# One more fp32 matmul per edge step on TensorE, ahead of the wait for the step's rows, in the passes of layers 1 to 3 of a four-layer graph network

## The chip, the cores and the metric

One core of one Trainium2 chip. The metric is the device time of one launch, in microseconds (us); lower is better.

## The reference, cut to what matters

A graph of 6250 nodes with 256 features and 100000 edges goes through four layers, each followed by a residual sum and a layer norm:

```python
x = _layernorm(x + _L0_gnn_ref(x, edge_index, ...))            # attention, 8 heads
x = _layernorm(x + _L1_gnn_ref(x, edge_index, ...))            # two GCN convolutions, 512 hidden
x = _layernorm(x + _L2_gnn_ref(x, edge_weight, ..., src, dst)) # edge-weighted convolution
x = _layernorm(x + _L3_gnn_ref(x, edge_index, edge_attr_2, ...)) # attention, 4 heads of 64
```

What matters here is the sum over edges in each layer: a row of a node table is fetched by the edge's source, weighted, and added to the row of the edge's destination.

```python
msg = h[src] * norm[:, None]
return jax.ops.segment_sum(msg, dst, num_segments=n_nodes) + b
```

The edges are sorted by destination. All arithmetic is float32.

## The kernel before, in words

Nodes are cut into 49 tiles of 128 (NODE_TILES). Edges are cut into 782 chunks of 128 (CHUNKS). A step pairs one chunk with one tile of destinations; since edges are sorted, 782 + 48 = 830 steps (STEPS) cover all pairs. The sums of all nodes lie in reg_acc, the features of all nodes in reg_x (as x_sb, tile by tile).

There are five passes over the edges. Layer 0 has its own (heads_*, product at L957); the change does not touch it. Layer 1 has two (edges1 and edges2) and layer 2 one (edges3); these three are instances of the class EdgePass (L1085 to L1152). Layer 3 has the last one (mix_*, L1494 to L1662). Dense layers and norms stand between the passes (close0 to close4), and each pass begins when the table that it gathers from has been stored.

One pass of EdgePass, engine by engine:

- POOL (L1099) issues one indirect DMA per chunk, 782 in all, each fetching 128 rows of 256 features into a ring of 60 slots. Gather j waits for the product of step j - 12 (AHEAD is 60 - 48 = 12), because a slot may be needed by up to 48 later steps.
- ACT (L1107) makes the one-hot matrix of a step (128 edges x 128 nodes) in two operations, four steps at a time (L1111 and L1116), in a ring of 12. In edges3 DVE makes it (L1136) with the edge weight in it.
- PE (L1118) multiplies: one fp32 matmul per step, one-hot x rows, 256 columns, into one of 8 PSUM banks (L1130). Before the product of step i it waits for the one-hot, for gather i (only if i < 782), and, from step 8 on, for the add of step i - 8, which frees the bank. The last 48 steps of a pass have no gather of their own.
- DVE (L1139) adds the bank into the tile's sums (L1152), each add behind the one before it.

The order of each engine is the order of its loop; nothing else schedules the work.

The last pass has 832 steps (STEPS_PAD), in 52 groups of 16:

- POOL (L1499) gathers rows of 136 columns by step, in a ring of three groups; gather t waits for the message of step t - 48.
- DVE at step i weights the message by head (L1651, after the product of step i - 4), mixes the message of step i + 1 (L1620), does a piece of the next group's score chain (chain, L1577; it begins by waiting for the last gather of the next group, L1583), and adds the product of step i - 2 to the sums (L1639). At the start of a group it rescales the sums (L1631 and L1633).
- ACT (L1555) makes the one-hots and the reversed messages and copies the weights.
- PE (L1517) does one product per step, 260 columns (L1526), into one of 6 banks, and two small operations per group for the running maximum (L1509, L1512). Before a product it waits for the one-hot, the weighted message, the weights, and the add of step i - 6.

An fp32 matmul leaves two records in the trace, so 830 products are 1660 records, and "x8" of PE's L153 or L1130 are four matmuls. A few records of PE are missing.

Of the kernel before, what the change touches and what calls it, by code (L numbers as in the profile page):

```python
# [46 lines left out]
EDGE_BANKS = 8  # L47
BANKS = 6
LAG = 2
ROW_OF_SLOTS = 32  # L50
NI, NF = 4, 3


# [159 lines left out]
def build(nc, io):  # L213
    ctx = ExitStack()
    with ctx:
        def sb(name, width, dt=F32, rows=P):
            return ctx.enter_context(nc.sbuf_tensor(name, [rows, width], dt))
# [21 lines left out]
        attr1 = sb("attr1", STEPS_PAD)  # L239
        step_rows = sb("step_rows", STEPS_PAD, I32, rows=ROW_OF_SLOTS + 1)  # L240
        tile_row, slot_row = step_rows[0:1, :], step_rows[ROW_OF_SLOTS:ROW_OF_SLOTS + 1, :]
        group_row = sb("group_row", NODE_TILES, I32, rows=1)
        ident = sb("ident", P)
# [4 lines left out]
        psum = [ctx.enter_context(nc.psum_tensor(f"bank{k}", [P, 512], F32)) for k in range(8)]  # L248
# [11 lines left out]
        x_sb = reg_x[:, 0:NODE_TILES * FEAT].rearrange("p (t f) -> p t f", f=FEAT)  # L260
# [381 lines left out]
        def load_slots(e, t0):  # L642
            if not slot_regs:
                slot_regs.extend(e.alloc_register(f"slot{k}") for k in range(GROUP))
            n = min(GROUP, STEPS - t0)
            e.load(slot_regs[0:n], slot_row[:, t0:t0 + n])

        def slot_rows(e, t):
            v = e.snap(slot_regs[t % GROUP], min_val=0, max_val=(SLOTS - 1) * FEAT)
            return scratch[:, bass.DynSlice(v, FEAT)]  # L650
# [428 lines left out]

        ring_rows = scratch[:, 0:SLOTS * FEAT].rearrange("p (s f) -> p s f", f=FEAT)
        ring_hots = scratch[:, SLOTS * FEAT:SLOTS * FEAT + HOTS * P].rearrange("p (s f) -> p s f", f=P)

        class EdgePass:  # L1085
# [32 lines left out]
            def tensor(self, e):  # L1118
                for i in range(STEPS):
                    if i % GROUP == 0:  # L1120
                        load_slots(e, i)
                    if self.weighted:
                        e.wait_ge(*self.hot(i))
                    else:
                        e.wait_ge(*self.hot4(i // 4))
                    if i < CHUNKS:
                        e.wait_ge(*self.got[i % AHEAD](i // AHEAD))
                    if i >= EDGE_BANKS:
                        e.wait_ge(*self.added(i - EDGE_BANKS))
                    e.matmul(psum[i % EDGE_BANKS][:, 0:FEAT], ring_hots[:, i % HOTS, :], slot_rows(e, i),  # L1130
                             start=True, stop=True).then_inc(*self.product.up)

# [345 lines left out]
        product3, added3 = s_edge.take(STEPS_PAD), s_added.take(STEPS_PAD)  # L1478
        scaled_3, denscaled3 = s_scaled.take(GROUPS - 1), s_denscaled.take(GROUPS - 1)

        def close3_over(e):

            e.wait_ge(*h3_stored.end)
            e.wait_ge(*src_by_step.end)
            e.wait_ge(*cleared_l2.end)
            e.wait_ge(*norm_l2.scaled.end)
            e.wait_ge(*dense_l3.turned.end)
            e.wait_ge(*taken_l3.end)
# [14 lines left out]
        def mix_tensor(e):  # L1503
            close3_over(e)

            def chain(g, k):
                if k == 4:
                    e.wait_ge(*cm_v.at("top", g))
                    e.transpose(top_bank[0:HEADS3, 0:P], top, ident[:, :]).then_inc(*cm_t.done("top"))  # L1509
                if k == 9:  # L1510
                    e.wait_ge(*cm_v.at("diag", g))
                    e.matmul(top_bank[:, 256:256 + HEADS3], ones4, diag, start=True,  # L1512
                             stop=True).then_inc(*cm_t.done("all"))

            for k in range(GROUP):
                chain(0, k)
            for i in range(STEPS_PAD):  # L1517
                g, k = i // GROUP, i % GROUP
                if g + 1 < GROUPS:
                    chain(g + 1, k)  # L1520
                e.wait_ge(*hot3(i // 4))
                e.wait_ge(*weighted3(i))
                e.wait_ge(*wkept3(i))
                if i >= BANKS:
                    e.wait_ge(*added3(i - BANKS))
                e.matmul(psum[i % BANKS][:, 0:WIDE3], hots3[:, i % 12, :], scaled3[:, i % 4, :], start=True,  # L1526
                         stop=True).then_inc(*product3.up)

# [217 lines left out]
        @block.tensor  # L1746
        def _(e):
            prep_tensor(e)
            heads_tensor(e)
            edges1.tensor(e)  # L1750
            close1_tensor(e)
            edges2.tensor(e)
            close2_tensor(e)
            edges3.tensor(e)
            close3_tensor(e)
            mix_tensor(e)
# [102 lines left out]
```

## Time and profile before

| | us |
|---|---|
| median of 3 runs | 6089.86 |
| lowest and highest of them | 6069.24, 6090.07 |
| the profiled execution's own time | 6087.99 |
| its span, first to last instruction | 6086.2 |

From the profiled execution, busy time and share of the span by engine:

| engine | busy us | share | instructions |
|---|---|---|---|
| PE (matmul) | 4655.6 | 76% | 13320 |
| POOL | 4038.2 | 66% | 4116 |
| DVE | 3512.5 | 58% | 10769 |
| ACT | 2590.8 | 43% | 7522 |

PE is TensorE's matmuls and PEld its weight loads; DVE is VectorE, ACT ScalarE, POOL GpSimd. Busy time of PE depends on its clock: the granted clock is given as a share of 2.4 GHz, so 1.00 is 2.4 GHz and 0.50 is 1.2 GHz; its mean over the span is 0.696. Matmuls overlap each other, and a record shows a matmul's whole way through the array; the distance between the starts of two tells the rate. In the timeline a line merges like instructions that follow each other closely, and the bracket behind it tells how long the engine was idle before it and what ended that.

The pass edges1 lies from 1375 to 2389 us, edges2 from 2609 to 3623, edges3 from 3746 to 4760, and the last pass from 4858 to 6002.

### The profile page before, as it was taken

To read this page: it belongs to the slowest core of one execution; us is meant where nothing else is said; L and a number is where in the kernel's file an instruction comes from. 1 tells how busy PE (TensorE), PEld (TensorE's weight loads), DVE (VectorE), ACT (ScalarE), POOL (GpSimd) and SP (SyncE) were. 2 spreads that over 40 slices of the span, in tenths; PEclk is the share of its full clock that TensorE was granted. 3 is DMA by queue.
4 is the path that set the end of the run, shared out by engine and by line. 5 is a ranking of instruction groups with operands and counts; after the bars stand their busy time and mean duration, and the time that the engine had idled before them with its cause. 6 is when DMAs were issued, how large, how long until landed. Compare 5 with 4: busy or idle time off the path is not lost.

```text
span 6086.2 us, 70752 instructions
## 1 busy us (share of the span) xinstructions
PE 4655.6 (76%) x13320; PEld 2535.9 (42%) x13320; DVE 3512.5 (58%) x10769; ACT 2590.8 (43%) x7522; POOL 4038.2 (66%) x4116
## 2 busy tenths in 40 slices
PE   5899988837888888988888863887888856666663
PEld 3667666623333334633333331333333623333331
DVE  4767787783333335833333347555555767777777
ACT  1655566554444444444444453000000456666664
POOL 2776677727777773067777755777777177777772
PEclk8877798775655667966565665656565977777776
DMA  4433343334333331033333322333333122222221
GB/s 128 107 106 96 96 107 107 101 96 119 105 105 106 106 105 50 33 105 106 106 105 105 106 62 82 105 106 105 105 105 105 36 54 53 53 53 53 53 53 55
DMA packets 237655, 539.07 MB, mean 89 GB/s; under 512 B 68266, under 2 KB 120424, under 8 KB 237242
## 3 DMA queue, kind: packets, MB, share of 16 engines
q0 software_dynamic: 180176, 481.36, 29.2%
q1 hardware_dynamic: 57066, 53.19, 2.7%
q8 instruction: 140, 2.29, 0.2%
q14 instruction: 273, 2.24, 0.1%
HBM read 498.15 MB, written 36.14 MB: 88 GB/s over the span
## 4 chain that ended last, share of the span: by engine, by line
PE 64%; issue 14%; DVE 12%; ACT 5%; POOL 2%; DMA 1%; DVEq 1%; ACTq 0%; POOLq 0%
PE bank L1130 40%; PE bank L1526 10%; PE bank L957 8%; PE bank L814 4%; PE bank L802 2%; DVE reg_acc L1152 1%; DVE scratch L183 1%; DVE scratch L201 1%; POOL scratch L1103 1%; DVE reg_acc L985 1%; ACT scratch L1541 1%; DVE scratch L1242 1%; ACT scratch L1546 1%; DVE scratch L1245 1%; DVE scratch L1233 1%
## 5 line engine op out<-in xcount | busy, mean ns | idle before, releaser
L1130 PE MATMUL bank<-scratch 128*128 x4980 | 2582.2, 634 | 668.3 <-issue 279.3
L1152 DVE TENSOR_TENSOR reg_acc<-reg_acc,bank 128x256 f32 x2490 | 1049.6, 422 | 1803.2 <-PE bank L1130 1779.7
L1130 PEld LDWEIGHTS bank<-scratch 128*128 128x128 f32 x4980 | 1147.9, 281 | 2102.5 <-issue 2077.3
L1103 POOL DMA_INDIRECT scratch<-tab_x,src_idx x1564 | 1479.5, 946 | 513.9 <-issue 383.8
L1111 ACT ACTIVATE scratch<-iota_row,dst_loc 128x128 f32<-128x128 f32 x1660 | 660.7, 401 | 1084.7 <-PE bank L1130 1066.0
L1103 POOL DMA_INDIRECT scratch<-tab_h,src_idx x782 | 739.3, 945 | 494.6 <-DMA tab_h<-reg_acc 256.7
L1499 POOL DMA_INDIRECT scratch<-tab_h,src_idx x832 | 856.1, 1029 | 263.8 <-issue 162.1
L710 POOL DMA_INDIRECT reg_x<-tab_h,src_idx x832 | 809.4, 973 | 301.0 <-issue 174.3
L1526 PE MATMUL bank<-scratch 128*128 128x260 f32 x1664 | 676.8, 525 | 425.9 <-issue 403.9
L957 PE MATMUL bank<-reg_x,scratch 128*128 128x265 f32 x1664 | 639.8, 495 | 102.3 <-DVE reg_x L994 60.5
L1526 PEld LDWEIGHTS bank<-scratch 128*128 128x128 f32 x1664 | 326.7, 242 | 743.4 <-issue 702.3
L146 ACT COPY scratch<-bank 128x256 f32<-128x256 f32 (+1 forms) x196 | 76.8, 416 | 1035.0 <-PE bank L138 1035.0
L957 PEld LDWEIGHTS bank<-reg_x,scratch 128*128 128x128 f32 x1664 | 317.2, 227 | 245.4 <-DVE reg_x L994 215.6
L985 DVE TENSOR_TENSOR reg_acc<-reg_acc,bank 128x265 f32 x832 | 355.0, 427 | 100.4 <-PE bank L957 87.0
L994 DVE TENSOR_TENSOR reg_x<-reg_x 128x256 f32<-128x256 f32 x832 | 349.8, 421 | 0.4 <-ACT reg_x L767 0.4
L1639 DVE TENSOR_TENSOR reg_acc<-reg_acc,bank 128x260 f32 x832 | 341.4, 410 | 9.4 <-DVE reg_acc L1633 7.7
L1651 DVE TENSOR_TENSOR scratch<-scratch 128x256 f32<-128x256 f32 x832 | 342.8, 412 | 0.0
L1541 ACT ACTIVATE scratch<-iota_row,dst_loc 128x128 f32<-128x128 f32 x832 | 320.5, 386 | 0.0
L1136 DVE TENSOR_SCALAR scratch<-iota_row,dst_loc,edge_w 128x128 f32<-128x128 f32 x830 | 291.8, 352 | 0.0
L1564 ACT COPY scratch<-scratch 128x4 f32<-128x4 f32 x832 | 152.4, 183 | 326.4 <-PE bank L1526 321.3
L1552 ACT ACTIVATE scratch<-scratch,attr 128x64 f32<-128x64 f32 x832 | 285.9, 344 | 1.0 <-issue 0.9
L814 PEld LDWEIGHTS bank<-adst,scratch 128*128 128x128 f32 x1664 | 269.4, 241 | 38.6 <-issue 32.4
(229 smaller groups left out, 4430.7 us busy)
## 6 DMA issues: line engine op xcount, KB each, us to landing
scratch<-tab_h,src_idx POOLq DMA_INDIRECT x1614, 2.7
scratch<-tab_x,src_idx POOLq DMA_INDIRECT x1564, 2.7
reg_x<-tab_h,src_idx POOLq DMA_INDIRECT x832
reg_x<-in_x SPq DMA_DIRECT2D x12, 896.0 KB, 11.0
tab_h<-scratch SPq DMA_DIRECT2D x7, 924.0 KB, 4.5
tab_x<-reg_acc SPq DMA_DIRECT2D x7, 896.0 KB
tab_h<-reg_acc SPq DMA_DIRECT2D x7, 896.0 KB
tab_x<-reg_x SPq DMA_DIRECT2D x7, 896.0 KB
```

Of the source, the lines that this page charges most:

```text
L710: e.indirect_dma_start(rows0[:, t % (3 * S), 0:ROW0], None, tab_h0, bass.IndirectOffsetOnAxis(ap=src_idx[:, t:t + 1], axis=0)).then_inc(*g ...
L814: m = e.matmul(bank_d[:, t % S * H:(t % S + 1) * H], hots_t[:, c % 2, n * P:(n + 1) * P], adst[:, bass.DynSlice(tile_value(e, "tensor", t) ...
L957: e.matmul(psum[i % BANKS0][:, 0:W0_ROW], hots0[:, i % (2 * S), :], rows0[:, i % (3 * S), :], start=True, stop=True).then_inc(*product0.up)
L985: e.tensor_tensor(v, v, psum[i % BANKS0][:, 0:W0_ROW], ALU.add).then_inc(*added0.up)
L994: e.tensor_tensor(v, v, bcast(row[:, FEAT:ROW0], 2, [P, H, D]), ALU.mult).then_inc(*weighted0.up)
L1103: e.indirect_dma_start(ring_rows[:, j % SLOTS, :], None, self.table, bass.IndirectOffsetOnAxis(ap=src_idx[:, j:j + 1], axis=0)).then_inc(* ...
L1111: e.activation(ring_hots[:, i % HOTS, :], iota_row[:, :], ACT.Abs, scale=-1.0, bias=dst_loc[:, i:i + 1]).then_inc(*self.far.up)
L1130: e.matmul(psum[i % EDGE_BANKS][:, 0:FEAT], ring_hots[:, i % HOTS, :], slot_rows(e, i), start=True, stop=True).then_inc(*self.product.up)
L1152: e.tensor_tensor(v, v, psum[i % EDGE_BANKS][:, 0:FEAT], ALU.add).then_inc(*self.added.up)
L1499: e.indirect_dma_start(rows3[:, t % (3 * GROUP), :], None, tab_h3, bass.IndirectOffsetOnAxis(ap=src_idx[:, t:t + 1], axis=0)).then_inc(*go ...
L1526: e.matmul(psum[i % BANKS][:, 0:WIDE3], hots3[:, i % 12, :], scaled3[:, i % 4, :], start=True, stop=True).then_inc(*product3.up)
L1541: e.activation(hots3[:, i % 12, :], iota_row[:, :], ACT.Abs, scale=-1.0, bias=dst_loc[:, i:i + 1]).then_inc(*far3.up)
```

## The change

Each step of the three EdgePass passes from step 8 on, and of the last pass from step 6 on, gets one more matmul on PE: the identity matrix times the first 384 columns of x_sb (the node features, resident and unchanged during a pass), written to the bank that the step's product then overwrites (start=True). Its result is taken by nobody. The wait for the bank (the add of 8 or 6 steps before) moves from last to first among the step's waits, so that the new matmul can run before the step's one-hot and rows are there. The constant FILL0 is not used.

```diff
 BANKS = 6
 LAG = 2
 ROW_OF_SLOTS = 32
+FILL = 384
+FILL0 = 160
...
+        def busy_beside(e, bank, rows):
+
+            e.matmul(bank, ident[:, :], rows.rearrange("p t f -> p (t f)")[:, 0:FILL], start=True, stop=True)
+
...
                 for i in range(STEPS):
                     if i % GROUP == 0:
                         load_slots(e, i)
+                    if i >= EDGE_BANKS:
+                        e.wait_ge(*self.added(i - EDGE_BANKS))
+                        busy_beside(e, psum[i % EDGE_BANKS][:, 0:FILL], x_sb)
                     if self.weighted:
                         e.wait_ge(*self.hot(i))
                     else:
                         e.wait_ge(*self.hot4(i // 4))
                     if i < CHUNKS:
                         e.wait_ge(*self.got[i % AHEAD](i // AHEAD))
-                    if i >= EDGE_BANKS:
-                        e.wait_ge(*self.added(i - EDGE_BANKS))
                     e.matmul(psum[i % EDGE_BANKS][:, 0:FEAT], ring_hots[:, i % HOTS, :], slot_rows(e, i),
                              start=True, stop=True).then_inc(*self.product.up)
...
                 if g + 1 < GROUPS:
                     chain(g + 1, k)
+                if i >= BANKS:
+                    e.wait_ge(*added3(i - BANKS))
+                    busy_beside(e, psum[i % BANKS][:, 0:FILL], x_sb)
                 e.wait_ge(*hot3(i // 4))
                 e.wait_ge(*weighted3(i))
                 e.wait_ge(*wkept3(i))
-                if i >= BANKS:
-                    e.wait_ge(*added3(i - BANKS))
                 e.matmul(psum[i % BANKS][:, 0:WIDE3], hots3[:, i % 12, :], scaled3[:, i % 4, :], start=True,
                          stop=True).then_inc(*product3.up)
```

## Rows read from the trace of the kernel before

**Rows 1.** The page: busy time by engine, and the chain by line.

```profile
PE 4655.6 (76%) x13320; PEld 2535.9 (42%) x13320; DVE 3512.5 (58%) x10769; ACT 2590.8 (43%) x7522; POOL 4038.2 (66%) x4116
...
PE bank L1130 40%; PE bank L1526 10%; PE bank L957 8%; PE bank L814 4%; PE bank L802 2%; DVE reg_acc L1152 1%; DVE scratch L183 1%; DVE scratch L201 1%; POOL scratch L1103 1%; DVE reg_acc L985 1%; ACT scratch L1541 1%; DVE scratch L1242 1%;
```

**Rows 2.** Stretches: length, busy time of each engine, granted clock, DMA share, GB/s.

```profile
core 0: us, PE busy (x) PEld busy (x) DVE busy (x) ACT busy (x) POOL busy (x), PEclk, DMA share, GB/s
1390.00:2350.00 960.00, 819.84 (x1537) 359.65 (x1537) 323.83 (x769) 426.52 (x960) 726.06 (x769) 0.60 0.37 105
1436.00:1444.00 8.00, 7.62 (x14) 3.39 (x14) 2.95 (x7) 3.52 (x9) 6.12 (x7) 0.50 0.39 110
1444.00:1452.00 8.00, 6.33 (x14) 2.40 (x12) 2.77 (x7) 3.77 (x9) 5.92 (x7) 0.73 0.36 100
2356.00:2389.50 33.50, 26.28 (x96) 15.79 (x95) 20.65 (x49) 18.88 (x47) 0.00 (x0) 0.96 0.00 1
2400.00:2590.00 190.00, 187.79 (x805) 128.30 (x804) 165.41 (x321) 91.45 (x225) 0.00 (x0) 1.00 0.09 30
```

**Rows 3.** Groups in 1390:2350: busy us, mean ns; idle before, releasers.

```profile
L1130 PE MATMUL bank<-scratch 128*128 x1537 | 820.6, 647 | 140.7 <-issue 102.6 <-ACT scratch L1116 13.1 <-DVE reg_acc L1152 7.5
L1103 POOL DMA_INDIRECT scratch<-tab_x,src_idx x769 | 727.0, 945 | 234.2 <-issue 185.2 <-PE bank L1130 49.0
```

**Rows 4.** Timeline (start, us), ends of passes 1 and 3: POOL and DVE.

```profile
2351.78 0.95 POOL L1103 DMA_INDIRECT scratch<-tab_x,src_idx  x1 [0.30 <-issue]
...
2356.11 0.42 DVE L1152 TENSOR_TENSOR reg_acc<-reg_acc,bank 128x256 f32 x1 [0.87 <-PE bank L1130]
...
2389.07 0.42 DVE L1152 TENSOR_TENSOR reg_acc<-reg_acc,bank 128x256 f32 x1 [0.22 <-DVE reg_acc L1152]
...
4722.70 0.95 POOL L1103 DMA_INDIRECT scratch<-tab_x,src_idx  x1 [0.30 <-issue]
...
4726.46 0.42 DVE L1152 TENSOR_TENSOR reg_acc<-reg_acc,bank 128x256 f32 x1 [0.57 <-PE bank L1130]
...
4759.88 0.42 DVE L1152 TENSOR_TENSOR reg_acc<-reg_acc,bank 128x256 f32 x1 [0.22 <-DVE reg_acc L1152]
```

**Rows 5.** Timeline of PE in the dense layer behind pass 1.

```profile
2451.10 1.94 PE L153 MATMUL bank<-reg_w,scratch 128*128 128x512 f32 x4
2452.88 0.38 PE L138 MATMUL bank<-ident,reg_acc 128*128 128x128 f32 x2
2453.10 1.89 PE L153 MATMUL bank<-reg_w,scratch 128*128 128x256 f32 x8
2454.83 0.60 PE L138 MATMUL bank<-ident,scratch 128*128 128x128 f32 x4
```

**Rows 6.** Timeline, one group of the last pass: DVE and PE.

```profile
5304.94 0.22 DVE L1583 TENSOR_TENSOR scratch<-scratch,attr 128x64 f32<-128x64 f32 x1 [4.30 <-DMA scratch<-tab_h,src_idx]
...
5309.23 1.21 PE L1526 MATMUL bank<-scratch 128*128 128x260 f32 x2 [0.95 <-issue]
...
5326.31 0.23 DVE L1583 TENSOR_TENSOR scratch<-scratch,attr 128x64 f32<-128x64 f32 x1 [4.83 <-DMA scratch<-tab_h,src_idx]
```

**Rows 7.** The gathers of the last pass, 4890:6000, as in rows 3.

```profile
L1499 POOL DMA_INDIRECT scratch<-tab_h,src_idx x807 | 832.5, 1032 | 245.9 <-issue 154.8 <-DVE scratch L1620 91.1
```

**Rows 8.** Timeline later in the same group: POOL, DVE and PE.

```profile
5315.34 1.30 POOL L1499 DMA_INDIRECT scratch<-tab_h,src_idx  x1 [0.30 <-DVE scratch L1620]
5315.41 0.41 DVE L1651 TENSOR_TENSOR scratch<-scratch 128x256 f32<-128x256 f32 x1
...
5316.78 0.68 PE L1526 MATMUL bank<-scratch 128*128 128x260 f32 x2 [0.19 <-issue]
...
5316.94 0.95 POOL L1499 DMA_INDIRECT scratch<-tab_h,src_idx  x1 [0.30 <-DVE scratch L1620]
5317.21 0.41 DVE L1651 TENSOR_TENSOR scratch<-scratch 128x256 f32<-128x256 f32 x1
```

**Rows 9.** Timeline of DVE, the last two groups: their first and last instruction.

```profile
5969.30 0.22 DVE L1583 TENSOR_TENSOR scratch<-scratch,attr 128x64 f32<-128x64 f32 x1 [4.32 <-DMA scratch<-tab_h,src_idx]
...
6001.12 0.43 DVE L1639 TENSOR_TENSOR reg_acc<-reg_acc,bank 128x260 f32 x1 [0.22 <-DVE reg_acc L1639]
```

## Prediction, made before the changed kernel was run

> **What bounds the kernel now.** I read five views in this order: the page's busy times and chain, a table of stretches, the groups inside one edge pass, the timeline at the ends of the passes, and one group of the last pass. The page shows PE busiest (76%), and 40% of the chain that ended last at its line L1130 alone [rows 1]. That invites the reading that the edge passes wait for PE, and that a faster PE clock would shorten them. The stretches show what is odd about PE: through 960 us of pass 1 it is 85% busy, but at a mean granted clock of 0.60, while in the dense layer behind it the clock is 1.00, that is 2.4 GHz against 1.2 GHz at 0.50 [rows 2]. So most of PE's busy time in the passes is slowness.
>
> Who paces the pass? In the same 960 us, POOL issues 769 gathers of 945 ns each, with 234 us of gaps: 961 us, all of it [rows 3]. POOL's period is 945 + 304 = 1.25 us per step, and its gap is 0.30 us whether the releaser is "issue" or PE. Step i needs gather i, so PE does one step per 1.25 us at either clock. Does POOL itself wait for PE? Gather j needs product j-12. The add of step 781 is the 49th from the end; in pass 3 it starts at 4726.46, 3.8 us behind its gather (4722.70), in pass 1 at 2356.11, 4.3 us behind (2351.78) [rows 4]. Product j-12 was thus there 12 x 1.25 - 4.3 = 10.7 us before gather j. PE may fall 10 us behind before POOL feels it. The chain puts these steps down to PE only because PE works last in each step.
>
> The 48 last steps of a pass have no gather. They run from 2356.11 to 2389.49 at 0.69 us, and DVE paces them: an add of 422 ns and 0.22 us before the next, while PE needs only 0.43 us for a product [rows 4, 5].
>
> **The change, part by part.** Passes 1 and 2 of layer 1 and the pass of layer 2 (830 steps each) and the last pass (832 steps) get one more fp32 matmul per step, ident against 384 columns, from step 8 on (step 6 in the last pass). The wait for a free bank moves ahead of it; it asks for the add eight (six) steps back, long done in the main stretch, so the move costs nothing: only the rows' waits come after it, and if the add were late, the product would wait for it in either order.
>
> Price of the added matmul: the trace has none of 384 columns, so I take it between its neighbours. At clock 1.00 four matmuls of 256 columns take 2453.10 to 2454.83, 0.43 us each; two of 512 take 2451.10 to 2452.88, 0.89 us each (two records to a matmul) [rows 5]. Midway: 0.66 us. Bounds: 0.64 (1.5 x 0.43) and 0.89. The step becomes 0.43 + 0.66 = 1.09 us at 2.4 GHz, 2.19 us at 1.2 GHz.
>
> Which clock? 1.09 of 1.25 us is 87% busy with columns. The clock stood at 0.96 and 1.00 where PE was 78% busy (the 48 last steps) and 99% (the dense layer); where it falls again and again, in the main stretch, PE's fast step fills only 0.43 of 1.25 us (35%) [rows 2, 3, 5]. At 0.50 a step of 2.19 us would leave PE no gap at all, and behind a stretch of 95% busy at 0.50 it rises now (1436:1444, then 0.73) [rows 2]. So I take 1.00, after some microseconds at the start of a pass, in which PE falls behind by 0.43 us per us; 7 us of that are 3 us of the 10 us of slack.
>
> (1) Main stretch of three edge passes, 782 gathers each: 1.09 < 1.25, POOL goes on pacing: 0. The cover is 0.16 us per step; if it were gone (a step of 1.30 us, say), each pass would lose 782 x 0.05 = 39 us.
>
> (2) The last 48 steps: no gather to hide behind. PE needs 1.09 where DVE needed 0.69: 48 x 1.09 = 52.3 us. From the last gather to the end of the last add it is now 37.7 us in pass 1 and 37.6 in pass 3 (pass 2, the same program, is taken as alike); with the change 3.8 + 52.3 + 0.4 = 56.5. Loss: 18.9 each, **+57 us** for three [rows 4, 5]. The bounds of the price (0.64, 0.89) give +54 and +90; I keep 0.66, as 256 columns are the nearest form.
>
> (3) Last pass, main stretch. A group of 16 steps takes 21.4 us (5304.94 to 5326.31); DVE waits 4.3 and 4.8 us of it for the next group's rows: POOL paces here too [rows 6]. PE's demand: the first three steps are DVE's own (4.3 us to the product at 5309.23), then, at 1.10 for 260 columns and the fill, 13 x 1.10 = 14.3, and some 0.8 for the two small operations of a group (less than two products): 19.4 us < 21.4. The product at 5309.23 takes 1.21 us, a later one of the same group (5316.78) 0.68: the clock is low at the start of the group, behind the idle gap [rows 6, 8]; if it still falls, three steps take 6.6 instead of 4.3 us and the group 21.7. That closes the gap ahead of the next group, so it should not happen each time. Taken as 0; bound +0.3 x 51 = +15 us.
>
> (4) POOL's own pace there. Gathers last 1032 ns on average, not 945 [rows 3, 7]. The timeline says why: the gather that starts 0.07 us ahead of DVE's L1651 (5315.34 and 5315.41) takes 1.30 us, the next one, 0.27 us ahead of it (5316.94 and 5317.21), takes 0.95 [rows 8]. That costs 0.087 x 16 = 1.4 us per group. DVE's step is 0.90 us there now (5315.41 to 5317.21, two steps) [rows 8]; paced by PE it would be 1.10. A gather then shifts by 0.15 us per step against L1651, and meets the bad zone (some 0.35 us wide, an estimate from the 0.35 us by which that one is stretched) about once in five, not once in two or three: 2.7 x 0.33 = 0.9 us per group, 0.5 less. Because the first steps keep DVE's rhythm I take 0.4: **-20 us**. Bounds: 0.9 less (-45) and 0.5 more (+25), since where two rhythms lock is chance. The Trainium skill (SBUF — State Buffer, "Who interferes with whom") says a DVE instruction with two inputs in SBUF contends with a GpSimd instruction that reads SBUF, but that a tensor_tensor should leave descriptor generation alone. This trace agrees with the first half (L1651 has both inputs in SBUF; beside L1152, with one in PSUM, gathers stay at 945 ns) and not with the second; by the second alone this term would be 0 and the sum +64.
>
> (5) The last two groups have no gathers behind them: 5969.30 to 6001.55, 32.3 us [rows 9]. Then 4.3 + 29 x 1.10 + 0.8 + 0.6 = 37.6, and 2.3 if the clock is low at the start, as at 5309.23 now: **+7 us** (+5 to +8).
>
> Sum: 57 + 7 - 20 = +44. The profiled execution took 6087.99 us, 1.9 below the median of the runs shown (6089.86); so 6132 for it, 6134 for the median, 0.7% more. Each of the three runs shown lies within 21 us of the others; about 0.5% (30 us) is what a measurement can tell from no change.
>
> **Rivals.** *POOL is freed (not slower).* The extra matmul spreads DVE's L1651 so far apart that hardly any gather is stretched. All of 1.4 us in 51 groups would give back 71 us: 6090 + 64 - 71 = 6083. It decides the sign against 0.5% from 34 us on (0.67 us per group). For it: phases lock, and 0.15 us of shift is small. Against: it needs more than half of all stretches to go. *PE becomes the bound.* If the fill costs 0.89 us, a step is 1.32 and the edge passes follow PE: 3 x 782 x 0.07 = 164, with 90 for the ends: about 6340. If the clock stayed at 1.2 GHz, 2.19 us per step would add 0.94 x 2346 = 2200 us; the rise at 95% load [rows 2] speaks against it. The mild form, the last pass at PE's pace, gives 6150 to 6190. *The clock was the cost.* If the passes followed PE's slow steps, 2.4 GHz would bring PE's product from about 1.0 to 0.43 us; but POOL's 1.25 us leaves nothing to win: 0, and the ends still cost: this ends in my forecast. *It does nothing,* the ends being paced by DVE still: PE's fill would have to fit in 0.69 - 0.43 = 0.26 us; no row lets 384 columns do that.
>
> **How the numbers follow.** Forecast (ends dominate, some relief at POOL): 0.70, slower. POOL freed: 0.20, of which 0.17 within 0.5% and 0.03 faster. PE the bound somewhere: 0.07, slower. Nothing: 0.03, same. So slower 0.77, same 0.20, faster 0.03. The range goes from term (4) at its bound, 6090 + 64 - 45 = 6109, a little into the first rival (6100), to the sum with +15 of (3), +15 for a dearer step at the ends and +5 of (4): 6090 + 64 + 35 = 6189, cut to 6185 for what is unlikely together.
>
> **What would show it.** Clock near 1.00 in all passes; PE about 88% busy in the main stretches; edge gathers still 1.25 us apart, 782 in 977 us; DVE's adds 1.09 us apart in the last 48 steps, 56 us from the last gather to the end; L1651 at 1.1 us distance and fewer gathers over 1.2 us; groups of 21.0 us. Wrong would be: gathers with gaps above 0.3 us released by PE; a clock of 0.50 in the middle of a pass; the ends still at 0.69 us.

## The result, and the profile after

The changed kernel took 6129.77 us (median of 9 runs, 6085.37 to 6154.74), the kernel before beside it 6089.86 (9 runs, 6069.24 to 6111.16): ratio 1.0054, 95% interval 1.0031 to 1.0078. It is slower by 40 us in the medians, 0.65%, or 0.3 to 0.8% by the interval. The forecast was 6134, slower, +44. The profiled execution took 6137.57 us, with a span of 6135.8 and a mean granted clock of 0.927.

The page of the changed kernel: busy time by engine (rows 1 are its counterpart), and the costliest groups.

```profile
PE 5275.6 (86%) x19904; PEld 3455.7 (56%) x19904; DVE 3572.2 (58%) x10769; ACT 2622.6 (43%) x7522; POOL 4016.5 (65%) x4116
...
L1086 PE MATMUL bank<-reg_x,ident 128*128 128x384 f32 x6584 | 2681.1, 489 | 59.8 <-issue 59.5
```

L1086 is the added matmul, L1137 the edge passes' product (L1130 before), L1109 and L1159 their gather and add (L1103, L1152). In the last pass L1534 is the product, L1506 the gather, L1591 the start of the score chain and L1659 the weighting (L1526, L1499, L1583 and L1651 before). PE has 620 us more busy time, and the program is 40 us longer.

The same kernel by stretches, columns as in rows 2: the main part of pass 1 (7 us longer than the stretch in rows 2), its last steps, and the last pass.

```profile
1400.00:2367.00 967.00, 914.62 (x3097) 551.59 (x3098) 327.27 (x777) 433.79 (x971) 731.28 (x774) 1.00 0.36 106
2371.00:2423.00 52.00, 51.39 (x192) 35.97 (x190) 20.50 (x49) 20.68 (x47) 0.00 (x0) 1.00 0.00 1
4970.00:6010.00 1040.00, 915.77 (x3322) 606.34 (x3320) 816.23 (x3028) 689.44 (x2678) 798.34 (x794) 1.00 0.21 54
```

The clock is 1.00 where it was 0.60 [rows 2]. Yet POOL issues 774 gathers in 967 us, 1.25 us apart, as before. In the last steps PE, which was busy for 26.28 of 33.5 us there, is now busy for 51.39 of 52.

The gathers and the products of pass 1 in 1400:2367, columns as in rows 3.

```profile
L1109 POOL DMA_INDIRECT scratch<-tab_x,src_idx x774 | 731.6, 945 | 235.7 <-PE bank L1137 134.0 <-issue 101.7
L1137 PE MATMUL bank<-scratch 128*128 x1554 | 499.9, 404 | 31.1 <-DMA scratch<-tab_x,src_idx 27.9 <-ACT scratch L1122 1.9 <-issue 0.2
```

POOL's gap is still 235.7 / 774 = 0.30 us, whoever is named as its releaser; a record of a product now lasts 404 ns instead of 647, and PE's waits are for the rows.

The ends of passes 1 and 3, timeline of POOL and DVE: last gather, add of step 781, last add [rows 4].

```profile
2367.03 0.95 POOL L1109 DMA_INDIRECT scratch<-tab_x,src_idx  x1 [0.30 <-PE bank L1137]
...
2370.87 0.42 DVE L1159 TENSOR_TENSOR reg_acc<-reg_acc,bank 128x256 f32 x1 [0.83 <-PE bank L1137]
...
2422.55 0.42 DVE L1159 TENSOR_TENSOR reg_acc<-reg_acc,bank 128x256 f32 x1 [0.66 <-PE bank L1137]
...
4772.85 0.95 POOL L1109 DMA_INDIRECT scratch<-tab_x,src_idx  x1 [0.30 <-issue]
...
4776.62 0.42 DVE L1159 TENSOR_TENSOR reg_acc<-reg_acc,bank 128x256 f32 x1 [0.52 <-PE bank L1137]
...
4828.30 0.42 DVE L1159 TENSOR_TENSOR reg_acc<-reg_acc,bank 128x256 f32 x1 [0.66 <-PE bank L1137]
```

From the last gather to the end of the last add it is 55.9 us in both, 37.7 and 37.6 before. The 48 steps take 51.68 us, 1.077 each; the wait in front of an add is 0.66 us and named PE, where it was 0.22 us and DVE's own.

Below, the program is cut at the first and last gather and the last add of each pass. "Ends" is the time from a pass's last gather to the end of its last add, for passes 1, 2 and 3 together. "Rest" is the span without layer 0's pass, in which the change touches nothing.

| kernel | layer 0's pass (clock) | gathers of passes 1 / 2 / 3 | ends | last pass, median group | rest |
|---|---|---|---|---|---|
| before | 1149.6 (0.81) | 976.3 / 976.3 / 977.1 | 112.8 | 1143.2, 21.47 | 4936.6 |
| after | 1164.7 (0.80) | 976.1 / 976.3 / 977.1 | 167.8 | 1126.2, 20.99 | 4971.1 |

So the change costs 34.5 us in the parts that it touches: +55.0 at the ends, -17.0 in the last pass, -3.6 between passes (behind passes 1 and 3 the next pass begins 1.8 us sooner after the last add; in the first 4 us of the dense layer behind pass 1 the clock is 1.00, where it was 0.50). The other 15 us by which these two profiled executions differ lie in layer 0's pass.

### The profile page after: what moved, and what is told of

Read it like the earlier page. It is cut to its first block, busy times and chain, and to the rows that moved or that the text cites. A ratio compares the mean times of both kernels' runs of the same rounds, so it can differ in the third digit from the quotient of the medians.

```text
span 6135.8 us, 82950 instructions
## 1 busy us (share of the span) xinstructions
PE 5275.6 (86%) x19904; PEld 3455.7 (56%) x19904; DVE 3572.2 (58%) x10769; ACT 2622.6 (43%) x7522; POOL 4016.5 (65%) x4116
## 4 chain that ended last, share of the span: by engine, by line
PE 70%; DVE 9%; DMA 7%; issue 6%; POOL 3%; ACT 2%; DVEq 0%; ACTq 0%; POOLq 0%
PE bank L1086 31%; PE bank L1137 19%; PE bank L959 8%; PE bank L1534 6%; DMA scratch<-tab_x,src_idx 4%; PE bank L816 4%; DMA scratch<-tab_h,src_idx 2%; PE bank L804 2%; POOL scratch L1109 2%; DVE scratch L185 1%; DVE scratch L203 1%; DVE reg_acc L987 1%; POOL reg_x L712 1%; DVE scratch L1249 1%; DVE scratch L1252 1%
## 5 line engine op out<-in xcount | busy, mean ns | idle before, releaser
L1086 PE MATMUL bank<-reg_x,ident 128*128 128x384 f32 x6584 | 2681.1, 489 | 59.8 <-issue 59.5
L1159 DVE TENSOR_TENSOR reg_acc<-reg_acc,bank 128x256 f32 x2490 | 1048.7, 421 | 1819.6 <-PE bank L1137 1817.5
L1137 PE MATMUL bank<-scratch 128*128 x4980 | 1604.5, 404 | 335.4 <-DMA scratch<-tab_x,src_idx 283.8
L1109 POOL DMA_INDIRECT scratch<-tab_x,src_idx x1564 | 1479.4, 946 | 513.9 <-PE bank L1137 264.7
L1137 PEld LDWEIGHTS bank<-scratch 128*128 128x128 f32 x4980 | 843.4, 190 | 1315.8 <-issue 1048.9
L1086 PEld LDWEIGHTS bank<-reg_x,ident 128*128 128x128 f32 x6584 | 1233.6, 190 | 279.7 <-issue 109.0
L1109 POOL DMA_INDIRECT scratch<-tab_h,src_idx x782 | 739.3, 945 | 511.1 <-DMA tab_h<-reg_acc 273.2
L1506 POOL DMA_INDIRECT scratch<-tab_h,src_idx x832 | 835.1, 1004 | 263.8 <-issue 143.5
L1534 PE MATMUL bank<-scratch 128*128 128x260 f32 x1664 | 511.6, 390 | 142.9 <-issue 135.9
L1534 PEld LDWEIGHTS bank<-scratch 128*128 128x128 f32 x1664 | 308.9, 191 | 397.0 <-issue 226.8
L1659 DVE TENSOR_TENSOR scratch<-scratch 128x256 f32<-128x256 f32 x832 | 344.3, 414 | 0.3
L1143 DVE TENSOR_SCALAR scratch<-iota_row,dst_loc,edge_w 128x128 f32<-128x128 f32 x830 | 328.5, 397 | 0.0
```

The costliest lines, as they stand in the source:

```text
L1086: e.matmul(bank, ident[:, :], rows.rearrange("p t f -> p (t f)")[:, 0:FILL], start=True, stop=True)
L1109: e.indirect_dma_start(ring_rows[:, j % SLOTS, :], None, self.table, bass.IndirectOffsetOnAxis(ap=src_idx[:, j:j + 1], axis=0)).then_inc(* ...
L1159: e.tensor_tensor(v, v, psum[i % EDGE_BANKS][:, 0:FEAT], ALU.add).then_inc(*self.added.up)
L1506: e.indirect_dma_start(rows3[:, t % (3 * GROUP), :], None, tab_h3, bass.IndirectOffsetOnAxis(ap=src_idx[:, t:t + 1], axis=0)).then_inc(*go ...
```

## Experiments

My theory: the fill is free where a gather paces the step, and costs at the ends, where no gather does; the gain in the last pass comes from DVE's L1659, which PE's pace spreads out in time, so that it stretches fewer gathers. The rivals: the end of a pass isn't the cost, but something in the main stretch is; and the gain in the last pass comes from the clock, not from the pace.

Four sets of runs were made, each on one chip with the kernel before beside it. On the chips of two sets the kernel before took 6101.36 and 6099.73 us, on those of the other two 6997.5 and 6996.24. The first set fell on the slower kind, so its kernels but mix_only were run again (names ending in _b).

### The change again

**after_b**: no edit.

> The changed kernel itself, as a control on the chip of this call (on the chip of the runs before, the kernel before took 6998 us, and DMA paused for 1.6 to 3.3 us every 13 us or so). If this chip is like the first one (kernel before near 6090): edge passes 976 us plus 56 us each, last pass 1126 us, about 0.7% over the kernel before. If it is like the second: each edge pass loses 18 us at its end and 15 to 20 us in its main stretch, and the last pass 70 us, so some 170 us or 2.4% over the kernel before.

Measured 6139.29 us (5 runs) against 6101.36 (14): 1.0064, interval 1.0037 to 1.0091. Gathers 976.1 / 976.2 / 976.9, ends 167.9, last pass 1126.3 with groups of 20.99, rest 4971.6: within half a microsecond of the first profile. Layer 0's pass took 1138.6 (clock 0.82), 26 us less than there. So these two executions differ in layer 0's pass alone, and "rest" is the measure for what follows.

### No fill where no gather hides it

**ends_off** and **ends_off_b** (the same kernel twice): the fill stops with the last gather.

```diff
-                    if i >= EDGE_BANKS:
-                        e.wait_ge(*self.added(i - EDGE_BANKS))
-                        busy_beside(e, psum[i % EDGE_BANKS][:, 0:FILL], x_sb)
+                    if i >= EDGE_BANKS:
+                        e.wait_ge(*self.added(i - EDGE_BANKS))
+                    if EDGE_BANKS <= i < CHUNKS:
+                        busy_beside(e, psum[i % EDGE_BANKS][:, 0:FILL], x_sb)
```

> The changed kernel without the extra matmul in the last 48 steps of the edge passes. My theory: 18 us less at the end of each edge pass than the changed kernel on the same chip, 55 us in all, and nothing else changed. On a chip like the first: 37.6 us from last gather to end, and 0.2 to 0.3% below the kernel before. Rival: the extra matmuls of the main stretch cost something too, and the total stays above the kernel before.

ends_off_b: 6073.14 us (10 runs) against 6101.36: ratio 0.9951, interval 0.9929 to 0.9973; the change in the same set took 6139.29. Its timeline at the end of pass 1, DVE, the last two adds:

```profile
2414.92 0.42 DVE L1160 TENSOR_TENSOR reg_acc<-reg_acc,bank 128x256 f32 x1 [0.22 <-DVE reg_acc L1160]
2415.57 0.42 DVE L1160 TENSOR_TENSOR reg_acc<-reg_acc,bank 128x256 f32 x1 [0.22 <-DVE reg_acc L1160]
```

The 0.22 us and the releaser of before are back. The last gather started at 2378.82, so this end takes 37.2 us; all three take 112.3. Gathers take 976.6 / 976.5 / 977.3, the last pass 1126.5, rest is 4919.3: 17.3 us under the kernel before, 51.8 under the changed one. The ends are the whole cost of the fill in the edge passes. This version beats both kernels, on this kind of chip.

On the slower chip the same kernel was 1.87% slower than the kernel before.

> The changed kernel, but in the three edge passes the extra matmul is left out of the last 48 steps. My theory: the ends are all that the edge passes pay. From the last gather of a pass to the end of its last add it is 37.6 us again, as before the change (56 us with it), in each of the three; the main stretches stay at 1.25 us per gather with the clock near 1.00; the last pass stays at 21.0 us per group. In all 55 us less than the changed kernel, so some 6075 us by its median, 0.2 to 0.3% below the kernel before (the last pass's 17 us). Rival: the extra matmuls of the main stretch cost something too (through the rows' landing or POOL's pace); then a pass from its first to its last gather is longer than 976 us, and the sum falls by less than 55.

ends_off: 7127.34 us (4 runs) against 6997.5 (7): 1.0187, interval 1.017 to 1.0204. This went the other way, and what stood in its way was looked for in the trace. Two pairs of neighbouring gathers on POOL in pass 2's time there:

```profile
2084.36 0.95 POOL L1109 DMA_INDIRECT scratch<-tab_x,src_idx  x1 [0.30 <-issue]
...
2087.64 0.94 POOL L1109 DMA_INDIRECT scratch<-tab_x,src_idx  x1 [2.33 <-remote]
...
2098.91 0.94 POOL L1109 DMA_INDIRECT scratch<-tab_x,src_idx  x1 [0.30 <-issue]
...
2102.24 0.95 POOL L1109 DMA_INDIRECT scratch<-tab_x,src_idx  x1 [2.39 <-PE bank L1138]
```

POOL issues at 1.25 us and stops in between: in pass 2, 112 of its gaps are over 1 us, in the median 12.5 us apart, and 18 of them over 2 us. In the DMA engines, 111 pauses of more than 1 us (209 us in sum) lie between the starts of packets of 4096 B in 1700:2700; ends_off_b, the same kernel on the first kind of chip, has none in such a stretch of pass 1, nor has the kernel before (edges512_b has five). A gather's rows are added some 15 us behind its issue, not 4.3. So the ring of 12 steps is nearly used up (a slack of 1.6 to 2.0 us in the median, not 10.7), and rows land in bursts. My reading, not tested by itself, is that behind a pause PE has work waiting, and a step of 1.077 us catches up more slowly than one of 0.43 to 0.7. The kernel before left no trace on a slower chip.

### The last pass alone

**mix_only** takes the fill out of the edge passes: the line with busy_beside in EdgePass.tensor is removed.

> No extra matmul in the edge passes, the changed last pass kept (the wait's new place kept everywhere). My theory: the edge passes are as before the change, 976 us from first to last gather at a clock of 0.60, and 37.6 us at the end; so the total equals that of the run without the extra matmuls at the ends, within 5 us: the clock of PE is worth nothing in the edge passes. The last pass is 17 us shorter than before. Rival (the high clock has a worth in the edge passes): this run is slower than the one without the extra matmuls at the ends by more than 5 us in the passes 1 to 3 together.

On the slower chip: 7070.44 us, 1.0103 (1.0086 to 1.012). Edge gathers take 1120 to 1122 us a pass, against 1137 to 1139 with the fill (ends_off): on a chip where rows land in bursts, the main stretch costs 17 us a pass after all. This expectation missed: the two kernels were to be equal within 5 us, and mix_only is 57 us the faster in the medians. The rest of the loss is in the last pass, below. On the first kind of chip mix160_b, next, has the same edge passes without a fill: gathers 976.4 / 976.2 / 977.6 us at clocks of 0.58 to 0.61 and ends 114.2, against 976.6 / 976.5 / 977.3 at 0.99 and 112.3 in ends_off_b. There the clock is worth 2 us at most in them, as the theory had it.

**mix160** and **mix160_b**: that, and a narrower fill in the last pass. It is to lift the clock without setting the pace.

```diff
-FILL = 384
+FILL = 160
```

> Extra matmul in the last pass alone, of 160 columns (PE's step 0.71 us at 2.4 GHz, under DVE's 0.87). On a chip like the first: theory A (PE's pace spreads DVE's L1651, and fewer gathers meet it) says groups of 21.4 us, as before the change; theory B (PE's higher clock) says 21.0 us. On a chip like the second: groups of 25.5 us again.

mix160_b (one run, 6137.32 us, of which 1197.7 are layer 0's pass at a clock of 0.76): rest 4937.8, where the kernel before has 4936.6. The gathers of its last pass, and the stretch, over 4970:6010, then the same gathers in the changed kernel:

```profile
L1505 POOL DMA_INDIRECT scratch<-tab_h,src_idx x780 | 803.4, 1030 | 237.7 <-issue 141.4 <-DVE scratch L1627 96.3
```

```profile
4970.00:6010.00 1040.00, 781.89 (x3261) 606.84 (x3262) 781.22 (x2973) 656.64 (x2620) 802.62 (x780) 0.86 0.22 53
```

```profile
L1506 POOL DMA_INDIRECT scratch<-tab_h,src_idx x794 | 799.2, 1007 | 242.0 <-issue 132.6 <-DVE scratch L1628 109.4
```

At a clock of 0.86 (0.77 before, in 4970:6010) groups stay at 21.44 us, the weightings of a group's second half 0.867 us apart as before, and gathers at 1030 ns. The changed kernel has them 1.06 us apart, gathers at 1007 ns and groups of 20.99. The whole last pass takes 1141.0 us, and 1140.9 in edges512_b below, which has no fill there and a clock of 0.75. So a clock raised that far gives nothing here, and the pace is what goes with the gain.

The place of the gain says the same. In most groups of the kernel before, five gathers are over 1.0 us, those beside the weightings of steps 0, 4, 7, 10 and 13. The changed kernel spreads the weightings from step 11 on (1.25, 1.12, 1.05, 1.08 and 1.08 us to the next, where it was 0.93, 1.07 and three times 0.87), not the earlier ones, and the long gather at step 13 is gone. Timelines of POOL and DVE, step 13 of a group in the kernel before:

```profile
5318.19 1.31 POOL L1499 DMA_INDIRECT scratch<-tab_h,src_idx  x1 [0.30 <-issue]
...
5318.28 0.41 DVE L1651 TENSOR_TENSOR scratch<-scratch 128x256 f32<-128x256 f32 x1
```

Steps 10 and 13 of a group in the changed kernel:

```profile
5291.23 1.29 POOL L1506 DMA_INDIRECT scratch<-tab_h,src_idx  x1 [0.30 <-DVE scratch L1628]
...
5291.30 0.41 DVE L1659 TENSOR_TENSOR scratch<-scratch 128x256 f32<-128x256 f32 x1
...
5294.08 0.95 POOL L1506 DMA_INDIRECT scratch<-tab_h,src_idx  x1 [0.30 <-DVE scratch L1628]
...
5294.53 0.41 DVE L1659 TENSOR_TENSOR scratch<-scratch 128x256 f32<-128x256 f32 x1
```

Over the pass, the time by which gathers exceed 0.945 us is 70.8 us before and 49.8 after. Of it, 17.3 and 1.6 us lie beside the weightings of the last five steps, where mix160_b has 21.0 and edges512_b 17.6. In the other eleven, where the clock rose as well and the distances stayed, but for the one that leads to step 0, it fell from 53.4 to 48.1. So 16 of the 21 us go with the pace, and at most 5 with the clock alone; a run at a clock of 1.00 with the old pace was not made. What stretches a gather is not pinned to L1659 either: in both kernels every gather over 1.0 us overlaps the mixing behind it too (L1628, 0.34 us later, its inputs also in SBUF), and those that meet the weighting alone stay under 0.97 us.

> Extra matmul in the last pass alone, with 160 columns in place of 384. PE's step is then 0.44 + 0.27 = 0.71 us at 2.4 GHz, under DVE's 0.87. Theory A (the last pass gained because PE paces DVE's L1651 at 1.1 us, so that fewer gathers meet it): with 160 columns DVE keeps its rhythm, and the groups last 21.4 us as before the change, whatever the clock does. Theory B (it gained through PE's higher clock): the clock is higher than 0.76 here too, and the groups last 21.0 us or so.

mix160 on the slower chip (one run): 7059.94 us. Last pass 1356.3 us, with 384 columns 1364.8 to 1369.7, and in the kernel edges512 below, which has no fill there, 1292.8. The rule of the first chip is turned round: by that one run without it, a fill in the last pass costs 63 to 77 us there.

### The cover taken away

**edges512** and **edges512_b**: 512 columns in the edge passes, none in the last pass.

```diff
-FILL = 384
+FILL = 512
...
                 if i >= BANKS:
                     e.wait_ge(*added3(i - BANKS))
-                    busy_beside(e, psum[i % BANKS][:, 0:FILL], x_sb)
```

> Extra matmul of 512 columns in the edge passes alone; PE's step is 1.26 to 1.32 us, just over POOL's 1.25 (in the run before, its last 48 steps took 1.27 us each). On a chip like the first: with 1.27 us per step PE is the bound, POOL waits for PE, gathers are 1.27 us apart once the 10 us of slack are gone: a main stretch of 976 + 782 x 0.02 - 10, so 980 to 985 us, and 70 us from the last gather to the end, plus up to 10 us of backlog; the last pass is as before the change (21.4 us per group, 1143 us in all).

Measured 6267.13 us (one run). Pass 1 in it, 1400:2350, and its gathers:

```profile
1400.00:2350.00 950.00, 950.00 (x2947) 559.73 (x2946) 309.98 (x737) 411.15 (x920) 703.67 (x745) 1.00 0.36 104
```

```profile
L1109 POOL DMA_INDIRECT scratch<-tab_x,src_idx x745 | 704.1, 945 | 246.6 <-PE bank L1137 155.2 <-issue 91.4
```

PE is busy for 950.00 of 950 us. The timeline has a step of PE every 1.29 us, and POOL follows, released by it:

```profile
2000.88 0.94 POOL L1109 DMA_INDIRECT scratch<-tab_x,src_idx  x1 [0.35 <-PE bank L1137]
...
2001.73 1.02 PE L1086 MATMUL bank<-reg_x,ident 128*128 128x512 f32 x2
...
2002.17 0.94 POOL L1109 DMA_INDIRECT scratch<-tab_x,src_idx  x1 [0.35 <-PE bank L1137]
...
2003.03 1.02 PE L1086 MATMUL bank<-reg_x,ident 128*128 128x512 f32 x2
```

Gathers take 996.5 / 997.0 / 997.1 us instead of 976, the ends 77.7 / 77.1 / 77.7 (a backlog of 15 us and 48 steps of 1.29). The direction was expected, the size missed, 980 to 985 for the gathers: at 1.29 us a step, 782 x 0.04 less the 10 of slack makes 997. The cover is real, and it ends somewhere between a step of 1.077 us and one of 1.29. Its first microseconds are eaten from the ring: gather j comes 10.7 us behind the add of step j - 12 in the kernel before, and 0.6 us here (medians).

> Extra matmul of 512 columns, in the edge passes alone; the last pass without it. It takes the cover away: PE's step is 0.43 + 0.89 = 1.32 us, over POOL's 1.25. My theory: PE becomes the pass's bound, adds are 1.32 us apart all through, POOL waits for PE (gaps above 0.30 us), a pass lasts some 830 x 1.32 = 1096 us and 8 more for its start, 87 more than before: 6345 us in all, at a clock of 1.00. The last pass: 21.4 us per group. Rival: the pass's pace is held by something between landing and product that leaves room for it; then gathers stay 1.25 us apart and only the ends grow (by 30 us each, 6180).

edges512 on the slower chip (one run): 7141.7 us; gathers 1139.6 / 1141.2 / 1136.4, ends 70 us each. My first price for a step, 1.32 us, was too high; it measured 1.27 there and 1.29 on the first kind. The pass of 1104 us that it expected took 1210 there, with the pauses, and 1074 on the first kind.

### A fill in layer 0's pass

That pass scatters with its clock, so these kernels put a fill there, ahead of its wait for the weighted message.

```diff
-                e.wait_ge(*weighted0(i))
                 if i >= BANKS0:
                     e.wait_ge(*added0(i - BANKS0))
+                    e.matmul(psum[i % BANKS0][:, 0:256], ident[:, :], adst[:, 0:256], start=True, stop=True)
+                e.wait_ge(*weighted0(i))
```

**heads256_only** has 256 columns there and no fill elsewhere.

> No extra matmul in the passes of layers 1 to 3 at all; one of 256 columns (identity times a resident table, result overwritten) in each step of layer 0's pass from step 4 on. Theory: there, and not in the other passes, PE's clock is what is waited for; 256 columns keep it up, as in the run with 256 before (clock 0.92, 1383 us, against 0.79 and 1466 without). On a chip like the second (kernel before near 6997): 1383 us for this pass, all else as before, 6915 us or 1.2% below the kernel before. On a chip like the first: POOL's pace would be 20.4 us per group, PE with 0.43 us more per step 20 to 21, so 1080 to 1100 us in place of 1139 to 1198, 6030 to 6040 us in all, some 1% below the kernel before. Rival: on a chip like the first, where rows land in time, PE has no room for 256 columns, and the pass takes 1150 us or more: no gain.

Measured 6121.28 us (12 runs, 6118.34 to 6125.55) against 6099.73 (17 runs, 6059.26 to 6143.11): 1.004, interval 1.0017 to 1.0063. Layer 0's pass takes 1172.7 us at a clock of 0.98, where the profile of the kernel before has 1149.6 at 0.81. The stretch 200:1250 of this kernel, then of the kernel before:

```profile
200.00:1250.00 1050.00, 1014.63 (x5861) 864.26 (x5859) 780.36 (x2595) 592.87 (x1683) 759.40 (x778) 1.00 0.38 102
```

```profile
200.00:1250.00 1050.00, 932.03 (x4412) 707.21 (x4412) 792.68 (x2648) 603.32 (x1716) 757.34 (x778) 0.82 0.38 101
```

PE is busy for 97% of the time at 1.00, and it gets fewer of DVE's instructions done (2595, not 2648) in the stretch: here the fill has no cover. A group of 16 steps, by DVE's adds, lasts 21.9 us nearly throughout; in the kernel before it is 18.4 at the high clock and up to 26.2 where the clock is low. So the theory's gain of 1% did not come, and its rival did: at the high clock the fill costs about what the low clock costs without it. What it buys is a steady clock: the runs lie within 7.2 us of each other, 84 in the kernel before. Another 10 us (rest 4946.7, against 4936.6 in a profile from another chip) lie in the other passes: gathers 978.6 / 978.6 / 979.8, ends 114.7. Why wasn't followed up.

**heads160** (160 columns there, 384 in the last pass but its last two groups, none in the edge passes), **heads64_mix448** (64 and 448) and **heads256_mix320** (256 and 320) were meant for the first kind of chip and fell on the slower one.

> Three edits together, each seen in its own stretch: no extra matmul in the edge passes; the extra matmul of the last pass left out of its last two groups; and a new one of 160 columns (identity times a resident table, result overwritten) in each step of layer 0's pass from step 4 on. Theory: layer 0's pass (1139 to 1198 us in the five traces so far, at a clock of 0.82 to 0.76, its code untouched) is paced by PE's clock: groups last 18 to 20 us at 2.4 GHz and 25 to 26 at 1.2 GHz. 0.27 us more per step keep the clock up; then all groups take some 20.4 us (POOL's 16 x 1.28), the pass 1070 us or so, and the runs scatter less. Rival: PE has no room there, and 0.27 x 832 us come on top of the pass: 1250 us or more. Last pass: 4 us less from the last gather to the end (35 us), groups of 21.0 us. Edge passes: 976 + 38 us. In all about 6010 us by the theory.

> Layer 0's pass with an extra matmul of 64 columns (0.11 us); the last pass with 448 columns in place of 384. Layer 0: if the clock still falls with so little, groups of 25 us remain in part, between the 1150 of before and the run with 160 columns. Last pass: PE's step is 0.44 + 0.76 = 1.20 us, under POOL's 1.25; PE needs 4.3 + 13 x 1.20 + 0.8 = 20.7 us per group. Theory A (L1651 and the gathers meet less often when their rhythms differ little): groups of 20.6 to 21.0 us. Rival: PE becomes the bound, groups of 21.3 us or more.

> Layer 0's pass with an extra matmul of 256 columns (0.43 us); the last pass with 320 columns. Layer 0: if PE's room is used up, the pass is longer than with 160 columns. Last pass: PE's step is 0.44 + 0.55 = 0.99 us, only just above DVE's 0.87 to 0.93, so DVE's rhythm changes by little; theory A says groups between 21.0 and 21.4 us, theory B (the clock alone) 21.0 as with 384.

Measured, in that order: 7137.64 (4 runs; 1.0197, 1.018 to 1.0214), 7259.1 (one) and 6977.79 (one), against 6996.24. Layer 0's pass took 1549.6 (clock 0.78), 1660.6 (0.68) and 1383.2 (0.92), against 1465.7 in ends_off (0.79), whose code for this pass is that of the kernel before, on another chip of the slower kind: the narrow fills cost 84 and 195 us there, the wide one gains 83. The clock goes along with it, but why the narrow ones lower it wasn't tested. The last passes with 384, 448 and 320 columns took 1361.8, 1364.0 and 1355.0 us, with groups near 25.6, so what was expected of them for the first kind stays untested. Neither 448 nor 320 columns in the last pass, nor 160 or 64 in layer 0's, has a run on the first kind of chip.

## Why the prediction was right

**What bounds the passes** was read rightly: POOL's 1.25 us. The page's 40% for L1130 was no limit, for the products' records became 38% shorter and the gathers' 976 us of a pass stayed to 0.2 us. The ring's slack, put at 10.7 us, is 10.7 in the median, 11.1 after. One sign was off: PE was to be 88% busy in the main stretch and shows 95% (914.62 of 967 us), because a record covers a matmul's whole way; by the distance of its steps it is 1.077 of 1.25, or 86%.

**The price.** 0.66 us for 384 columns, midway between its neighbours; the step of 1.077 us leaves 0.64 for it, the lower bound, three halves of 256 columns. The neighbour of 512 columns was the worse guide: in edges512_b, fill and product together take 1.29 us, 0.86 for the fill and not 0.89.

**Term by term.** (1) Main stretches: 0 forecast, 0.0 to -0.2 measured. edges512_b shows that the cover was needed. (2) The last 48 steps: +57 forecast, +55.0 measured, and ends_off_b takes 55.5 of it back by that alone. (The prediction's 0.69 us a step before is not 0.42 + 0.22, which is 0.64: 44 of 48 waits in pass 1 are 0.22 us, three are 0.93.) (3) PE in the last pass's groups: 0 forecast; the wait for the next group's rows fell from 4.3 us and more to 3.4, so POOL still paces:

```profile
5280.78 0.27 DVE L1591 TENSOR_TENSOR scratch<-scratch,attr 128x64 f32<-128x64 f32 x1 [3.40 <-DMA scratch<-tab_h,src_idx]
...
5301.78 0.26 DVE L1591 TENSOR_TENSOR scratch<-scratch,attr 128x64 f32<-128x64 f32 x1 [3.42 <-DMA scratch<-tab_h,src_idx]
```

That is DVE's timeline of the changed kernel, and a group of 21.00 us. (4) POOL's own pace: -20 forecast, -21 measured up to the last gather. The direction and its ground, the pace, hold for 16 of the 21 us by the steps in which they lie. That the size came out is partly luck, for the working doesn't hold: a bad zone of 0.35 us in a distance of 1.10 is one gather in three, not one in five, and 2.7 of 16 is one in six; one in three at 0.33 us each would be 1.7 us per group, more than the 1.4 of before. The picture was too simple as well: L1659 is spread only from step 11 of a group on; before them DVE's other work sets its own rhythm, and the gain is one meeting less of five. Gathers over 1.0 us went from 31% to 24%, those over 1.2 us from 180 to 95 of 832. (5) The last two groups: +7 forecast. From the first L1591 of rows 9 to the end of the last add it was 32.3 us; the same two points are now 36.5 apart, +4:

```profile
6014.65 0.22 DVE L1591 TENSOR_TENSOR scratch<-scratch,attr 128x64 f32<-128x64 f32 x1 [2.85 <-DMA scratch<-tab_h,src_idx]
...
6050.68 0.43 DVE L1647 TENSOR_TENSOR reg_acc<-reg_acc,bank 128x260 f32 x1 [0.66 <-PE bank L1534]
```

The 2.3 us for a low clock at their start did not come: the clock no longer falls between groups. (6) Not foreseen: the dense layers behind passes 1 and 3 start at the high clock, -3.6.

Sum +34.5, against +44; the difference is 3 us in (5), 3.6 in (6), 2 in (2) and 1 in (4). That the median came within 4 us of the forecast is partly luck: layer 0's pass alone moves by more than that from run to run.

**The rivals.** POOL freed: the gain in the last pass stayed at 21 of 71 us. PE the bound: not at 384 columns, but edges512_b is that rival, at 1.29 us a step. The clock was the cost: at 1.00 instead of 0.60 the edge passes gained nothing in their gathers. It does nothing: the ends went from 0.69 to 1.077 us a step. By the Trainium skill (SBUF — State Buffer, "Who interferes with whom") a tensor_tensor should not slow descriptor generation; the Trainium skill marks that as inferred, and by it the last pass would not have gained through L1659. The measurement decides for the pair of L1659 and L1628: the gathers gained 21 us, and those that overlap both still take up to 1.44 us in the changed kernel, the others 0.94 to 0.97. The two instructions are not told apart.

**Open:** what pauses the DMA on the slower chips; why a fill costs 63 to 77 us in the last pass there; whether L1659 or L1628 stretches a gather; and whether 256 columns in layer 0's pass alone pay on the slower kind, where they took 83 us off that pass beside a costly fill in the last one.

## What to carry to other kernels

Before paying for a faster clock, find the engine whose period sets the pace, and check whether work by the slow engine would be finished sooner if it were faster; a share of the chain isn't that. Work put into a wait is free only in the steps that have the wait: look for the steps at a loop's end that lack it, and guard the filler with the same condition as the wait (here `i < CHUNKS`, worth 66 us in the medians and 52 without the scatter of layer 0's pass). Try it on more than one chip, since a cover of 0.17 us per step held on one kind and not on the other.

## What the runs showed of the hardware that was not expected

- The same program takes 6059 to 6143 us on some chips and 6992 to 7005 on others. Packets of 4096 B take as long on both (219 to 226 ns on average, and 220 to 221, in 1000 us or so of the edge passes); on the slower ones the starts of packets pause for more than 1 us 87 to 124 times in 1000 us, in traces of kernels with a fill.
- Layer 0's pass took 1138.6, 1149.6, 1154.4, 1164.7, 1177.6 and 1197.7 us at mean clocks of 0.82, 0.81, 0.81, 0.80, 0.78 and 0.76, with the same code. It seems to make nearly all of the scatter between runs: that is 84 us in the kernel before, and 7 with 256 more columns per step of this pass and a clock of 0.98.
- A fill can lower a clock: 64 and 160 columns in layer 0's pass went with 0.68 and 0.78, 256 with 0.92 (0.79 with none), all on the slower chips.
- An fp32 matmul of 384 columns costs 0.64 us at 2.4 GHz and one of 512 columns 0.86, each alternating with one of 256, by steps of 1.077 and 1.29 us with 0.43 us for the product.
- A gather of the last pass that overlaps DVE's weighting and mixing together takes 1.03 to 1.07 us on average and up to 1.44; one that overlaps neither, or the weighting alone, 0.94.
